# Expert shares in the sorted rows, adding gathers and three expert groups per slot in a retention-and-experts kernel

## The reference

```python
xn = _layernorm(x, axis=-1)
x = x + attn(xn, ...) + ffn(xn, Wg, We, be)

# attn: 4 layers of block(h, p)
r = _retention(h, wk)                 # k, q, v from h; tril(q k^T) / row_norm, divided by a clipped row sum; times v
a, gate = split(r @ w1 + b1, 2)
m = a * silu(gate) @ w2 + b2
y = _groupnorm1(m, gg, gb) + h        # mean and variance over the whole sequence
f = gelu(y @ wf1 + bf1_) @ wf2 + bf2_
h = _layernorm(f + y, lg, lb)

# ffn: 8 experts, 2 per token
topw, sel = top_k(xn @ Wg.T, 2);  topw = softmax(topw)
out = sum over the two chosen experts of topw * (We[e] @ xn + be[e])
```

## Time and profile before

| | us |
|---|---|
| median of 3 runs (480.22 to 485.19) | 480.33 |
| the profiled execution, by its own clock outside | 481.61 |
| its span, from the first to the last instruction | 479.8 |
| busy: PE, DVE, ACT, POOL | 423.3, 370.8, 282.7, 255.9 |
| mean granted clock of TensorE, share of full speed | 0.959 |

### The profile page before, as it was taken

How to read it: one execution, slowest core, us unless ns; L and a number is a source line. 1 busy time by engine, 2 the same in 40 slices (tenths; PEclk the granted TensorE clock), 3 DMA queues, 4 the chain that set the end, 5 groups by cost and what they waited for, 6 DMA issues and landing times.

```text
span 479.8 us, 8596 instructions
## 1 busy us (share of the span) xinstructions
PE 423.3 (88%) x2386; PEld 324.1 (68%) x2386; DVE 370.8 (77%) x1226; ACT 282.7 (59%) x579; POOL 255.9 (53%) x292
## 2 busy tenths in 40 slices
PE   8999679988987999999999999999999999866740
PEld 7977556766765777777887887777777676643320
DVE  6858897877766888677666666778889999997656
ACT  2943256656564666666777676666676666553321
POOL 4692217788887784212222222123268877777774
PEclk9999898999999999999999999999999999997785
DMA  8793001121111113344434444100001111211123
GB/s 247 229 283 106 0 2 44 39 78 40 38 40 38 40 44 90 84 114 123 123 106 115 126 122 115 58 23 1 1 24 39 37 30 34 55 52 55 55 60 94
DMA packets 57375, 36.05 MB, mean 75 GB/s; under 512 B 4544, under 2 KB 55280, under 8 KB 57328
## 3 DMA queue, kind: packets, MB, share of 16 engines
q1 hardware_dynamic: 53152, 27.09, 19.8%
q0 software_dynamic: 4096, 8.40, 6.0%
q10 hardware_dynamic: 80, 0.02, 0.0%
HBM read 19.23 MB, written 16.25 MB: 74 GB/s over the span
## 4 chain that ended last, share of the span: by engine, by line
PE 58%; DVE 22%; POOL 10%; issue 7%; ACT 2%; DVEq 0%; ACTq 0%; POOLq 0%
PE bank L329 6%; POOL sorted_rows L1375 5%; PE pair L435 5%; PE pair L428 4%; PE bank L520 4%; PE pair L410 4%; PE bank L524 4%; PE bank L491 4%; PE bank L565 3%; PE pair L437 3%; PE bank L418 3%; POOL picked L1384 2%; PE bank L321 2%; PE bank L325 2%; DVE x_in L1240 2%
## 5 line engine op out<-in xcount | busy, mean ns | idle before, releaser
L1405 POOL TENSOR_TENSOR ln_r<-ln_v,minus_half 128x4 f32<-128x4 f32 x32 | 33.2, 1038 | 102.7 <-ACT ln_v L836 102.4
L1375 POOL DMA_INDIRECT sorted_rows<-va,rows_of x64 | 64.0, 1000 | 20.3 <-issue 20.3
L1384 POOL DMA_INDIRECT picked<-sorted_results,rows_of x64 | 64.1, 1002 | 17.8 <-issue 15.9
L1415 POOL TENSOR_TENSOR y_part<-y,y_part 128x512 fp32r<-128x512 f32 x32 | 41.8, 1305 | 38.5 <-ACT y_part L811 38.5
L804 ACT ACTIVATE hg<-vt,gn_c,g_prev 128x512 f32<-128x512 f32 x32 | 26.0, 814 | 52.5 <-DVE gn_c L1199 52.5
L435 PE MATMUL pair<-va,scores 128*128 128x129 f32 x256 | 49.3, 297 | 6.5 <-DVE scores L1115 4.9
L1115 DVE TENSOR_TENSOR scores<-pair,const 128x512 f32<-128x512 f32 x32 | 22.0, 688 | 39.3 <-PE pair L428 39.3
L844 ACT ACTIVATE va<-bank,ln_off,ln_r 128x128 f32<-128x128 f32 x128 | 48.2, 457 | 1.1
L321 PE MATMUL bank<-ot,b_w 128*128 128x512 f32 x64 | 40.1, 626 | 6.8 <-DVE past L1109 3.7
L435 PEld LDWEIGHTS pair<-va,scores 128*128 128x128 f32 x256 | 38.7, 204 | 7.3 <-DVE scores L1115 5.5
L321 PE MATMUL pair<-y_part,f_w 128*128 128x512 f32 x64 | 39.2, 612 | 0.0
(11 more groups left out here) (176 smaller groups left out, 1137.7 us busy)
## 6 DMA issues: line engine op xcount, KB each, us to landing
sorted_rows<-picked SPq DMA_DIRECT2D x9, 512.0 KB, 6.5
sorted_x<-sorted_rows SPq DMA_DIRECT2D x18, 256.0 KB, 3.1
tile_w<-expert_rows_t SPq DMA_DIRECT2D x72, 64.0 KB, 1.8
sorted_results<-result SPq DMA_DIRECT2D x18, 256.0 KB, 2.4
x_in<-in_L_attn_x_dram SPq DMA_DIRECT2D x8, 256.0 KB, 5.0
out_dram<-x_in SPq DMA_DIRECT2D x8, 256.0 KB, 2.3
wf<-in_L_attn_Wf_dram SPq DMA_DIRECT2D x2, 512.0 KB, 6.1
sorted_rows<-va,rows_of POOLq DMA_INDIRECT x64
```

What stands on the lines that cost most here:

```text
L1375: pool.indirect_dma_start(sorted_rows[:, :], bass.IndirectOffsetOnAxis(ap=rows_of[:, j, n:n + 1], axis=0), va0[:, k, c, 0:D], None).then_i ...
L1384: pool.indirect_dma_start(picked[:, n % PICKED, j, :], None, sorted_results[:, :], bass.IndirectOffsetOnAxis(ap=rows_of[:, j, n:n + 1], ax ...
L1415: pool.tensor_tensor(y_part[:, 1, :], y[:, n % 2, :], y_part[:, 0, :].bitcast(F32), ALU.subtract).then_inc(y_rest, 1)
```

## The change

Shares: a sorted row becomes 130 numbers wide. Number 128 is a one, and number 129 is the token's share of that expert; the scatters run in two passes, first all first choices (with the first share, copied in by `put_first_share`), then all second choices (after `put_second_share`, which waits until the first pass has landed). The product of a group is multiplied by the row's share when it leaves PSUM, now on VectorE. Gathers no longer fill `picked`: each adds its rows to `x_in` in the transfer itself, in two passes, the second after the first has landed. `combine` is gone. Loads have three buffers and wait for the result of the group three before; three groups share a slot, in slots 17 to 23; scatters come six per slot. `rest_of_y` moves to VectorE. The eight bias products stand in slots 12 to 19. The order in all four `slot` functions is written anew, items stand one slot later in some stages, and the banks of PSUM are dealt out otherwise, with their waits. Its core:

```diff
-    PICKED = 4
+    DEEP = 3
+    BLANK = 6
-        sorted_x = sb("sorted_x", P, 2, GROUP, D)
+        sorted_x = sb("sorted_x", P, DEEP, GROUP, AUG)
...
-            for h in range(TILES // 8):
-                sp.dma_start(sorted_rows[h * 8 * P:(h + 1) * 8 * P, :].rearrange("(j p) d -> p j d", p=P), blank).then_inc(blanked, 16)
+            for h in range(TILES // BLANK):
+                sp.dma_start(sorted_rows[h * BLANK * P:(h + 1) * BLANK * P, :].rearrange("(j p) d -> p j d", p=P), blank.rearrange("p (j d) -> p j d", d=AUG)).then_inc(blanked, 16)
...
             def load_group(g):
-                if g >= 2:
-                    sp.wait_ge(tiles_done, g - 1)
+                if g >= DEEP:
+                    sp.wait_ge(results_set, g - DEEP + 1)
...
-            load_group(0)
-            load_group(1)
+            for g in range(DEEP):
+                load_group(g)
             for g in range(GROUPS):
                 rows_in_group = sorted_results[g * GROUP * P:(g + 1) * GROUP * P, :]
                 sp.wait_ge(results_set, g + 1)
                 sp.dma_start(rows_in_group.rearrange("(j p) d -> p j d", p=P), result[:, g % 2, :, :]).then_inc(group_out[g % 2], 16)
-                if g + 2 < GROUPS:
-                    load_group(g + 2)
+                if g + DEEP < GROUPS:
+                    load_group(g + DEEP)
```

TensorE's slot after the change, whole in its order but for the early slots' extras:

```diff
+                step(turn_v, n - 10, 0, 24)
+                step(turn_o, n - 3)
+                step(feed_b, n - 6)
+                step(turn_tiles, 3 * (n - 18) + 2, 0, GROUPS)
+                step(ask_tiles, 3 * (n - 18), 0, GROUPS)
+                step(project, n - 2)
+                step(route_bias, n - 12, 0, 8)
+                step(mix_out, n - 4)
+                step(ask_tiles, 3 * (n - 18) + 1, 0, GROUPS)
+                step(mix_gate, n - 3)
+                step(mix_a, n - 3)
+                step(ask_tiles, 3 * (n - 18) + 2, 0, GROUPS)
+                step(back_b, n - 6)
+                step(back_a, n - 6)
+                step(score, n - 2)
+                step(group_mean, n - 4)
+                step(gram, n - 1)
+                step(turn_tiles, 3 * (n - 17), 0, GROUPS)
+                step(attend_first, n - 2)
+                step(attend_second, n - 2)
+                step(attend_rest, n - 2)
+                step(feed_a, n - 5)
+                step(turn_tiles, 3 * (n - 17) + 1, 0, GROUPS)
+                step(turn_z, n - 6)
```

VectorE, GpSimd:

```diff
+            def put_first_share():
+                dve.wait_ge(share_step, 2)
+                dve.tensor_copy(shares, total[:, 1, :].rearrange("p (k c) -> p k c", c=C)).then_inc(share_put, 1)
+            def put_second_share():
+                dve.wait_ge(tile_step, TILED)
+                dve.wait_ge(scattered, 16 * CHUNKS)
+                dve.tensor_copy(shares, second_share[:, :].rearrange("p (k c) -> p k c", c=C)).then_inc(share_put, 1)
+            def set_results(g):
+                dve.wait_ge(tiles_done, g + 1)
+                if g >= 2:
+                    dve.wait_ge(group_out[g % 2], 16 * (g // 2))
+                dve.tensor_tensor(result[:, g % 2, :, :], TILE_OUT_BANK[:, :].rearrange("p (j d) -> p j d", d=D),
+                                  sorted_x[:, g % DEEP, :, D + 1].unsqueeze(2).to_broadcast((P, GROUP, D)), ALU.mult).then_inc(results_set, 1)
+            def rest_of_y(n):
+                dve.wait_ge(y_rounded, n + 1)
+                dve.tensor_tensor(y_part[:, 1, :], y[:, n % 2, :], y_part[:, 0, :].bitcast(F32), ALU.subtract).then_inc(y_rest, 1)
...
             def scatter(n):
-                k, c = divmod(n, C)
+                j, i = divmod(n, CHUNKS)
+                k, c = divmod(i, C)
+                if i == 0:
+                    pool.wait_ge(share_put, j + 1)
                 pool.wait_ge(*normalised(k))
-                for j in range(2):
-                    pool.indirect_dma_start(sorted_rows[:, :], bass.IndirectOffsetOnAxis(ap=rows_of[:, j, n:n + 1], axis=0),
-                                            va0[:, k, c, 0:D], None).then_inc(scattered, 16)
+                pool.indirect_dma_start(sorted_rows[:, :], bass.IndirectOffsetOnAxis(ap=rows_of[:, j, i:i + 1], axis=0),
+                                        va0[:, k, c, :], None).then_inc(scattered, 16)
             def gather(n):
...
-                read(pool, n, x_added, PICKED)
-                for j in range(2):
-                    pool.indirect_dma_start(picked[:, n % PICKED, j, :], None, sorted_results[:, :],
-                                            bass.IndirectOffsetOnAxis(ap=rows_of[:, j, n:n + 1], axis=0)).then_inc(picked_in[n % PICKED], 16)
+                if n == CHUNKS:
+                    pool.wait_ge(first_added, 16 * CHUNKS)
+                pool.wait_ge(bias_set, k + 1)
+                pool.indirect_dma_start(x_in[:, k, c, :], None, sorted_results[:, :],
+                                        bass.IndirectOffsetOnAxis(ap=rows_of[:, j, i:i + 1], axis=0),
+                                        compute_op=ALU.add).then_inc(x_added[k] if j else first_added, 16)
```

More of the change, by code:

```diff
@@ L700, in _ @@
+                if n == -30:
+                    pe.wait_ge(xt_set, 1)
+                    turn_params(banks[4])
+                step(turn_z, n - 6)
+                if n == 2:
+                    turn_in(4, banks[4])
+                if n == 4:
+                    pe.wait_ge(xt_set, 8)
+                    ask_gate(6, banks[3])
+            for n in range(-83, 38):
                 slot(n)
@@ L954, in _ @@
+                step(norm_veps, n - 4)
+                step(round_y, n - 2)
+                step(set_gt, n + 1)
+            for n in range(-58, 37):
                 slot(n)
@@ L1341, in slot @@
[L1341 to L1352 removed]
+                step(add_biases, n - 11, 0, 8)
+                step(scale_last, n - 8, 24)
@@ L1353, in slot @@
+                if n == 10:
+                    place_tiles(banks[6])
+                step(set_results, 3 * (n - 17) + 1, 0, GROUPS)
+                step(group_stats, n - 3)
+                if n == 5:
+                    set_route()
+                if n == 16:
+                    rest_of_b(3, banks[6])
+                step(group_aggr, n - 3)
+                if n == 4:
+                    rest_of_b(1, banks[1])
+                if n == 5:
+                    put_first_share()
                 step(group_means, n - 3)
-            for n in range(-50, 40):
+            for n in range(-63, 41):
@@ new lines, in slot @@
+                step(group_factor, n - 73)
+                if n == -27:
+                    in_factor(2)
+                step(gather, 6 * (n - 93) + 2, 0, 64)
+                step(scatter, 6 * (n - 75) + 2, 0, 64)
+                if n == -25:
+                    in_factor(3)
+                step(gather, 6 * (n - 93) + 3, 0, 64)
+                step(gather, 6 * (n - 93) + 4, 0, 64)
+                if n == 46:
+                    shift_x(3)
+                    shift_x(4)
+                step(scatter, 6 * (n - 75) + 3, 0, 64)
@@ L1468, in slot @@
                 if n == -9:
                     in_factor(6)
+                step(scatter, 6 * (n - 74) + 1, 0, 64)
+                step(norm_factor, n - 75)
+                if n == -2:
                     shift_x(0)
[L1471 to L1477 removed]
@@ L1478, in slot @@
-                step(scatter, 4 * (n - 38) + 3)
-                if n == -10:
-                    in_factor(3)
-            for n in range(-42, 71):
+                if n == -28:
+                    in_factor(1)
+                if n == 51:
+                    split_biases()
+                if n == -18:
+                    in_factor(5)
+                if n == 2:
+                    shift_x(2)
+                if n == 77:
+                    shift_x(7)
+                if n == 51:
+                    shift_x(5)
@@ L1483, in _ @@
+            for n in range(-36, 107):
                 slot(n)
```

710 lines of the change are left out of this document (318 added, 392 removed).

## The result

| | before | after |
|---|---|---|
| median, us | 481.52 (4 runs) | 503.96 (4 runs) |
| ratio to before | 1 | 1.045, 95% interval 1.0377 to 1.0523 |
| span of the profiled execution, us | 479.8 | 502.4 |

A forecast was written before the change was run, and what follows sets the result against it. SP's issues and the loop behind them were to bound the group stage. Terms: 479.8 + 38 (groups) - 9 (scatters) + 2 (router) - 3 (VectorE) - 13 (drain) = 494.8 us of span, so 495 us, range 468 to 512.

The forecast's parts named there:

- Groups, +38: Expert-group stage: three groups per slot make SP's loads and the loop behind them take 21.2 us against TensorE's 14.8; +38 us.
- the upper bound: Group stage: with turn and product at half clock, 2 us per turn more, +48 instead of +38.
- SP only paces: Rival, group stage: latencies overlap and only SP's issue rate counts, +11 in place of +38, 468 us; chance 0.04.
- Fetching transfers, "nothing, up to +3": Adding fetches on GpSimd: 64 issues still at 1.3 us, landing between a gather's and twice that; nothing, up to +3 us.
- Scatters, -9: Seven scatter slots: six scatters and no `rest_of_y` put GpSimd under a slot, 84 instead of 93.5 us; -9 (-13 to 0).
- The wait between passes: Scatters: the second pass's wait for the first's landing is covered by GpSimd's other work; if not, some 3 us, once.
- Router, +2: Router stretch: nearly full VectorE gets more work, while GpSimd's 1.3 us for `rest_of_y` leaves the path; +2 us (0 to +4).
- Drain, -13: End of the kernel: `combine` leaves the path, `rest_of_y` gets shorter, five slots at about 2.7 us less; -13 (-20 to -6).
- the far bound: Drain: -20 us, with all of the expected saving.
- VectorE becomes the bound: Rival: `rest_of_y` in VectorE's queue makes its loop 11.8 instead of 11.3 us in some 16 slots, 503 us; chance 0.12.
- Loads hide: Rival, group stage: SP needs at most 3.6 us per group, so +38 falls away, 457 us; chance 0.14.
- Transfers crawl: Rival, adding fetches: each must land (2.5 us) before the next starts, 40 us more than planned, some 535 us; chance 0.05.

The follow-up runs named there:

- The fixed expert: The change with each tile's weights loaded from an expert fixed in advance, so SP reads no number into a register: 462.18 us, ratio 0.9542 to the kernel before.
- the exchanged order: The change with TensorE's first product of a burst put ahead of the third turn: 484.79 us, ratio 1.0021 to the kernel before.
- the run without addition: The change with fetching transfers that overwrite instead of adding, same count, sizes, waits and order: 479.25 us, ratio 0.9887 to the kernel before.
- the run with eight: The change with eight scatters per slot instead of six, starting two slots later: 516.76 us, ratio 1.0688 to the kernel before.

## Why the prediction was right, step by step

**Groups, +38: measured +43.7, for the reason given.** The working had a turn of 21.2 us: 17.0 for three loads, 1.5 of landing, 1.93 of turn and product, 0.7 of result. The five turns of the trace take 22.2 on average: 17.9, 1.5, then 2.1 from the turn's start to the result's, and 0.7. So the term that was short is SP's time for three loads, by 0.9 us per turn. The product at half clock, which only the upper bound held, came in two turns of five (2.7 and 2.9 us from turn to result, where the other three had 1.6), and on average the term is 0.1 above the working. The five turns make 4.8 of the 5.7 us that the stage took beyond the forecast, the start-up and the rest 0.9. The fixed expert and the exchanged order each took away a part, by 41 and 17 us of the stage. With the exchange the stage still cost +26.6 and not the +11 of "SP only paces": that figure had 17.0 for SP, left out the start-up, and took the loop as gone.

**Fetching transfers, "nothing, up to +3": the step that failed.** "From below it costs what a gather does" named the landing, and the 64 issues were left at 1.3 us each. The landing did go up within its bounds (3.3 us; 2.5 in the run without addition), but it is not what counted: the hold of GpSimd per transfer rose by 0.59. The nine slots became 116.0 us instead of the 102.1 that come from 105.1 - 3, and in the run without addition they were 99.7. The same hold kept the end at 55.3, where that run had 46.8. GpSimd's slot should have been added up for the fetches as it was for the scatters. The Trainium skill, page "Perfetto Trace Analysis", section "DMA Instruction — SWDGE (GPSIMD)", says that such an instruction's end in a profile is the end of writing descriptors and not of moving data. The trace agrees as to the two being different things: 1.59 us of GpSimd beside 3.3 us to the landing.

**Scatters, -9: measured -14.7.** The mechanism held (slots of 11.0 to 11.9 us, TensorE's own: it is busy 77.9 of the 78 us from 76 to 154), and the share of eight against six is shown by the run with eight. Mis-sized were 0.3 us of waiting per slot and 5 us of extras, which mostly found room. The move of `rest_of_y`, put down as part of the gain, gives nothing here (0.9 us) and is worth 11 us only beside the adding fetches. The wait between passes cost nothing, as said, but "some 3 us" without cover was too little: 9.64 in the run with eight.

**Router, +2: measured -6.3.** The working priced what VectorE gets and not which of TensorE's waits the new order drops. The waits of TensorE before, 16 to 82 us, and after, 16 to 76:

```profile
PE bank L321 <- DVE past L1109: 3.1, 1, 3.1
PE bank L399 <- DVE rows_of L1052: 3.0, 1, 3.0
```

```profile
PE pair L325 <- DVE ot L1158: 2.4, 2, 2.2
```

Two waits of 3 us are gone. That the order alone did this is argued from the traces; no run tried it.

**Drain, -13: measured -11.** Near, but by two misses against each other: without the additions it would have been -19.5, close to the far bound, and the additions took 8.5 of it back. The signs named for it did not come: `mix_out` was 12.8 us apart and not 10 to 11, and GpSimd's fetches set the pace at the end.

**Sum.** Against the forecast by stage: -8.3 before item 5, -5.7, +5.7, +13.9, +2.0, together +7.6 of the 502.4 - 494.8. The largest miss and the two gains nearly cancel, so the total is nearer than its terms. That is luck: with the misses of the groups, the fetches and the drain alone, the span would have been 516 us, and the time beyond the range's 512. The direction and the largest term, the groups, are not luck.

**The rivals.** "VectorE becomes the bound" had the right total (503) for the wrong reason: in the run without additions, with the same work on VectorE, TensorE shows no wait at all from 331 to 430 us. "Loads hide" (457) had about the right price, as the fixed expert showed (a span of 461.6, still with adding fetches), but its condition, at most 3.6 us of SP per group, did not hold: 5.8. "Transfers crawl" was right in its kind, an addition that costs something, and not in its place: the transfers overlap (3.3 us to landing at a step of 1.9), GpSimd's holds don't. The Trainium skill says on page "DMA: Bandwidth & Descriptors", section "Issuing engines are not separate DMA queues", that the time on the sequencer to start a DMA is usually small beside the DMA itself. The trace disagrees for this stage: with the read it is 1.1 us of SP from tile to tile, beside 1.9 to the landing, and it is the bound.

## What to carry to other kernels

Put more pieces of work into a slot only after adding up the queue that issues their transfers, with its register reads; where a load waits for a result and the result's product waits behind the last load's turn, count the whole turn of that loop and look for one exchange that opens it. Loads that depend on early data belong into the time in which their queue is idle. A transfer that does arithmetic is not free for the engine that issues it: price the issuing engine, not only the landing.

## What was not expected of the hardware

- An indirect transfer that adds holds GpSimd for 1.59 us against 0.97 for one that overwrites the same rows, and lands after 3.3 us against 2.5.
- An adding transfer of the same bytes makes 112 packets more (11264 packets in GpSimd's queue against 4096, over 64 such transfers).
- Reading an expert's number into a register and issuing with it takes SP 1.1 us from tile to tile, where the issue with a fixed address takes 0.5. The read alone is 0.27 us, and in the turn shown 0.60 directly behind a load of rows.
- A wait on TensorE can be paid twice: in two turns of five the granted clock stood at 0.50 behind the waits, and the product took 1.91 us instead of 1.06.
